# Two routed stages' last expert done tile by tile, their sums read back inside the stage, shared weights as a ninth expert, rows transposed inside the next stage, first modulations loaded early

## What is computed

```python
gates = softmax(x_flat @ router_w + router_b)
_, topk_idx = top_k(gates, 2)                       # 8 experts, capacity 320 tokens each
buf = ...                                           # the tokens of each expert
h = gelu(einsum('ecd,edh->ech', buf, w1) + b1)      # 256 -> 1024
out = einsum('ech,ehd->ecd', h, w2) + b2            # 1024 -> 256
y = einsum('ned,ne->nd', gathered, weights)         # back to the tokens, weighted and summed
```

```python
gate_in = concat([full_agg, hp_agg, wp_agg])        # three means over parts of the sequence
gate_scores = softmax((gate_in @ gate_w + gate_b) * (1 + scale) + shift)
topk_w, topk_i = top_k(gate_scores, 2)
out = sum over e of w_be[:, e] * mask[e] * (gelu(c @ ew1[e] + eb1[e]) @ ew2[e] + eb2[e])
out = out + gelu(c @ sw1 + sb1) @ sw2 + sb2         # the shared expert
```

## Time and profile before

| what | value |
|---|---|
| median of three runs | 2343.88 us (2343.78 to 2346.67) |
| span of the profiled execution | 2341.6 us (the profile gives no other time of it; the median is 2.3 us more) |
| TensorE busy | 2027.8 us, 87% of the span |
| DVE busy | 1336.4 us, 57% |
| ScalarE busy | 981.6 us, 42% |
| GpSimd busy | 370.6 us, 16% |
| instructions | 33811 |

### The profile page before, as it was taken

The page is one execution under the profiler, slowest core; times in us unless marked ns, Lnnn a source line. Parts: engine busy times, 40 slices in busy tenths (PEclk is TensorE's granted clock), DMA queues, the critical chain, the costliest instruction groups (busy, mean ns, idle before and its releaser), DMA issues. The chain is left out here.

```text
span 2341.6 us, 33811 instructions
## 1 busy us (share of the span) xinstructions
PE 2027.8 (87%) x13199; PEld 1631.2 (70%) x13199; DVE 1336.4 (57%) x2445; ACT 981.6 (42%) x1942; POOL 370.6 (16%) x308
## 2 busy tenths in 40 slices
PE   6699699999899999999999895499946767698698
PEld 3499578888687888888888784388933555366465
DVE  2766447777674465474463213666527457365796
ACT  2235445655453454454454322145323336455332
POOL 1368101323100000000000002257720000000000
PEclk7799799999999999999999997699977866899899
DMA  2654212233014112111200110544345002010000
GB/s 82 221 158 121 49 37 95 88 107 105 6 39 119 33 40 61 33 39 61 35 14 10 38 42 2 171 145 114 80 98 156 2 2 55 18 55 3 0 10 27
DMA packets 111160, 150.45 MB, mean 64 GB/s; under 512 B 6856, under 2 KB 93431, under 8 KB 110616
## 3 DMA queue, kind: packets, MB, share of 16 engines
q1 hardware_dynamic: 99836, 130.14, 18.6%
q0 software_dynamic: 11168, 18.18, 3.9%
HBM read 124.08 MB, written 24.22 MB: 63 GB/s over the span
## 5 line engine op out<-in xcount | busy, mean ns | idle before, releaser
L1750 DVE TENSOR_TENSOR m_h_lo<-m_hf,m_h_hi 128x512 fp32r<-128x512 f32 x256 | 173.8, 691 | 310.9 <-ACT m_hf L1725 307.1
L1722 ACT ACTIVATE m_h_hi<-m_h_ps,m_bT 128x512 fp32r<-128x512 f32 x256 | 177.0, 691 | 366.8 <-PE m_h_ps L396 347.0
L641 POOL DMA_INDIRECT token_sums<-e_y,slot_row x56 | 183.8, 3282 | 104.8 <-DVE e_y L749 84.4
L1725 ACT ACTIVATE m_hf<-m_h_ps,m_bT 128x512 f32<-128x512 f32 x256 | 175.0, 684 | 0.0
L711 ACT ACTIVATE e_h_hi<-e_h_ps,e_b1T 128x320 fp32r<-128x320 f32 (+1 forms) x128 | 77.9, 609 | 163.1 <-PE e_h_ps L396 158.0
L1435 DVE TENSOR_TENSOR c_h_lo<-c_hf,c_h_hi 128x512 fp32r<-128x512 f32 x120 | 91.9, 774 | 87.5 <-ACT c_hf L1391 86.8
L772 DVE TENSOR_TENSOR e_h_lo<-e_hf,e_h_hi 128x320 fp32r<-128x320 f32 (+1 forms) x128 | 72.3, 582 | 112.0 <-ACT e_hf L714 112.0
L1284 POOL TENSOR_TENSOR cT<-cT,c_yg 128x128 f32 x88 | 77.3, 879 | 265.1 <-DVE c_yg L1453 252.0
L1388 ACT ACTIVATE c_h_hi<-c_h_ps,c_b 128x512 fp32r<-128x512 f32 x88 | 62.2, 706 | 106.5 <-PE c_h_ps L396 105.9
L396 PE MATMUL m_y_ps<-m_h_hi,l_w_1hi 128*128 128x512 f32 x256 | 100.3, 392 | 3.4 <-issue 3.4
L396 PE MATMUL m_y_ps<-m_h_hi,l_w_0hi 128*128 128x512 f32 x256 | 99.8, 390 | 1.4 <-ACT m_gT L1736 1.4
(11 more groups left out here) (664 smaller groups left out, 5446.2 us busy)
## 6 DMA issues: line engine op xcount, KB each, us to landing
cT<-in_L_ffn_W_dram SPq DMA_DIRECT2D x30, 1024.0 KB, 5.2
res<-in_L_cond_ew_dram SPq DMA_DIRECT2D x22, 1024.0 KB, 5.0
cT<-in_L_ffn_w_dram SPq DMA_DIRECT2D x16, 1024.0 KB, 5.6
res<-gates_rows SPq DMA_DIRECT2D x8, 1024.0 KB, 15.5
l_mod<-modulation_rows SPq DMA_DIRECT2D x16, 512.0 KB, 6.5
token_rows<-d_tok SPq DMA_DIRECT2D x2, 2112.0 KB, 10.2
token_sums<-res SPq DMA_DIRECT2D x2, 2048.0 KB, 7.5
res<-token_sums SPq DMA_DIRECT2D x8, 512.0 KB, 7.2
```

What stands on the lines that cost most here:

```text
L641: pool.indirect_dma_start(out=sums, out_offset=bass.IndirectOffsetOnAxis(ap=st.slot_row[0:r, e, j:j + 1], axis=0), in_=y[0:r, e % 2, j, :] ...
L1722: act.activation(hs[0][:, f, :], h_ps[:, f % HB, :], ACT.Relu, bias=bT[:, at:at + 1])
L1725: act.activation(hf[:, f % HB, :], h_ps[:, f % HB, :], ACT.Relu, bias=bT[:, at:at + 1]).then_inc(act_done, 1)
L1750: dve.tensor_tensor(hs[1][:, f, :], hf[:, f % HB, :], hs[0][:, f, :].bitcast(F32), ALU.subtract).then_inc(h_ready, 1)
```

## The change

The last expert (e = 7) of both routed stages is multiplied down tile by tile, in the order 0, 2, 1, 3; each tile is scaled and scattered as it is finished. SyncE issues the loads of the sums inside the routed stage's block, behind its wait for the last scatter. In `e0` the shared expert's weights become a ninth expert's: they are loaded into the raw buffers and split by DVE during the last expert, like any next expert's. The small loads of layer 1, and ScalarE's Silu and the load of its Gelu table, move to that block too. `l1_turn_phase` is gone: TensorE transposes the first block of rows ahead of the first unit, and the other three inside its `up`, behind groups 1, 3 and 5, into PSUM banks from which ScalarE and DVE copy them. Means and choice, the count, the lists and their spreading come later, in the order that the diff shows. In `e3` the raw buffers take the first four chunks of modulations (`FirstModulations`), as they come free during the last two experts; `l3_phase` then starts with the weights.

```diff
     def load_w1(self, sp, e):
-        sp.dma_start(self.w1[e % 2], self.W1[e].rearrange("(c p) f -> p c f", p=P)).then_inc(self.w1_in[e % 2], 16)
+        W1 = self.W1[e] if e < E8 else self.shared[0]
+        sp.dma_start(self.w1[e % 2], W1.rearrange("(c p) f -> p c f", p=P)).then_inc(self.w1_in[e % 2], 16)
...
     def load_w2(self, sp, e):
-        sp.dma_start(self.w2[e % 2], self.W2[e].rearrange("(c p) d -> p c d", p=P)).then_inc(self.w2_in[e % 2], 16)
+        W2 = self.W2[e] if e < E8 else self.shared[1]
+        sp.dma_start(self.w2[e % 2], W2.rearrange("(c p) d -> p c d", p=P)).then_inc(self.w2_in[e % 2], 16)
...
+    E_ALL = E8 + following.experts
+    tile_order = [j for j in range(0, J, 2)] + [j for j in range(1, J, 2)]
...
+    order_of = lambda e: range(J) if e + 1 < E8 else tile_order
...
-            for e in range(2, E8):
+            for e in range(2, E_ALL):
                 sp.wait_ge(w1_split, 2 * (e - 1))
                 raw.load_w1(sp, e)
                 sp.wait_ge(w2_split, 2 * (e - 1))
                 raw.load_w2(sp, e)
-            if shared:
-                shared.load(sp, w1_split, w2_split)
+            sp.wait_ge(b_turned, 1)
+            following.load(sp, st, w1_split, w2_split)
+            back.load(sp, st)
...
-                for j, (_, r) in enumerate(tiles):
-                    pool.wait_ge(scaled, e * J + j + 1)
+                for i, j in enumerate(order_of(e)):
+                    r = tiles[j][1]
+                    pool.wait_ge(scaled, e * J + i + 1)
                     pool.indirect_dma_start(out=sums, out_offset=bass.IndirectOffsetOnAxis(ap=st.slot_row[0:r, e, j:j + 1], axis=0),
                                             in_=y[0:r, e % 2, j, :], in_offset=None, compute_op=ALU.add).then_inc(y_out, 16)
...
+
+                def products(f, j):
+                    a, r = tiles[j]
+                    for i, (h, w) in enumerate(((0, 0), (0, 1), (1, 0))):
+                        last = pe.matmul(y_ps[0:r, j // 2, j % 2, :], hs[h][:, f, a:a + r], w2s[e % 2][w][:, f, :],
+                                         start=False, stop=(f == FC - 1 and i == 2), skip_group_check=True)
+                    return last
+
+                if e + 1 < E8:
+                    for f in range(FC):
+                        pe.wait_ge(h_ready, e * FC + f + 1)
+                        for j in range(J):
+                            last = products(f, j)
+                    last.then_inc(y_done, 1)
+                else:
+                    for i, j in enumerate(tile_order):
+                        if i >= 2:
+                            pe.wait_ge(scaled, e * J + i - 1)
+                        for f in range(FC):
+                            if i == 0:
+                                pe.wait_ge(h_ready, e * FC + f + 1)
+                            last = products(f, j)
+                        last.then_inc(y_done, 1)
...
+            following.prepare(act, st)
...
-                dve.wait_ge(y_done, e + 1)
-                for j, (_, r) in enumerate(tiles):
+                for i, j in enumerate(order_of(e)):
+                    r = tiles[j][1]
+                    if i == 0 or e + 1 == E8:
+                        dve.wait_ge(y_done, e + i + 1)
                     if e >= 2:
                         dve.wait_ge(y_out, 16 * (e - 1) * J)
                     dve.tensor_scalar(y[0:r, e % 2, j, :], y_ps[0:r, j // 2, j % 2, :], taken[0:r, e % 3, j, D + e:D + e + 1],
...
             for e in range(E8):
-                more = e + 1 < E8
+                more = e + 1 < E_ALL
...
+                if e + 1 < E8:
+                    rows_lo(e + 1)
                 if more:
-                    rows_lo(e + 1)
                     w2_low(e + 1, 0)
                     w2_low(e + 1, 1)
             scale(E8 - 1)
...
+    def prepare(self, act, st):
+        act.activation(self.act_cond[:, :, :], st.condT[:, :, :], ACT.Silu)
+        act.activation(self.warm[:, :], st.ones[:, 0:1], ACT.Gelu_apprx_tanh)
...
-def l1_turn_phase(nc, sem, st, src, dst, back, shared, small, w1, w2):
...
-            def up(u):
+            def turn(b):
+                pe.wait_ge(back.res_in[b], 16)
+                if b >= 2:
+                    pe.wait_ge(rows_kept, b - 1)
+                for c in range(KC):
+                    for j in range(TPB):
+                        last = pe.transpose(y_ps[:, b % 2, c, j * P:(j + 1) * P], st.res[:, b * TPB + j, c * P:(c + 1) * P],
+                                            st.ident[:, :])
+                last.then_inc(rows_turned, 1)
...
+                    if f in between:
+                        between[f]()
...
+                if u == 0:
+                    pe.wait_ge(late_kept, 1)
...
+            turn_biases()
+            turn(0)
+            up(0, {1: lambda: turn(1), 3: lambda: turn(2), 5: lambda: turn(3)})
             down(0)
-            pe.wait_ge(selected, 1)
-            pe.matmul(ps[:, 0, 0:E4], st.ones[0:B, :], chosen[:, :], start=True, stop=True, skip_group_check=True)
-            pe.matmul(ps[0:B, 0, E4:2 * E4], st.tri[0:B, 0:B], chosen[:, :], start=False, stop=True,
-                      skip_group_check=True).then_inc(counted, 1)
-            up(1)
-            pe.wait_ge(listed, 1)
-            for e in range(E4):
-                last = pe.matmul(ps[:, 1, 0:2 * ROUTED * SLOTS], st.ones[0:B, :], hot[:, e, :, :].rearrange("b w s -> b (w s)"),
-                                 start=(e == 0), stop=(e == E4 - 1))
-            last.then_inc(spread, 1)
+            gate_logits()
+            up(1, {4: count_chosen})
+            pe.wait_ge(counts_kept, 1)
+            down(1)
+            up(2, {2: spread_list})
             pe.wait_ge(columns_set, 1)
-            down(1)
-            for u in range(2, UNITS):
+            down(2)
+            for u in range(3, UNITS):
                 up(u)
...
+            act.wait_ge(rows_turned, 1)
+            act.activation(xs[0][0][:, :, :], y_ps[:, 0, :, :], ACT.Copy).then_inc(x_hi, 1)
             act.wait_ge(b_kept, 1)
+
+            def keep_rows(b):
+                act.wait_ge(rows_turned, b + 1)
+                act.activation(srcT[:, :, blk(b)], y_ps[:, b % 2, :, :], ACT.Copy).then_inc(late_kept, 1)
...
+                    if u == 0 and f == 4:
+                        keep_rows(2)
+                    if u == 0 and f == 6:
+                        keep_rows(3)
...
-            dve.tensor_scalar(agg[:, 1:3, :, :], agg[:, 1:3, :, :], with_proprio, None, ALU.mult).then_inc(agg_done, 1)
+            keep_rows(0)
...
+                if f == 1:
+                    keep_rows(1)
             x_low(1)
...
+            means()
+            choose()
...
+                if f == 3:
+                    keep_counts()
+            list_slots()
             x_low(2)
...
-            for u in range(2, UNITS):
+            for f in range(FC):
+                h_low(2, f)
+                if f == 0:
+                    out_shared(1)
+                if f == 4:
+                    set_columns()
+            x_low(3)
...
+    experts = 0
...
+    def load(self, sp, st, w1_split, w2_split):
+        for c in range(4):
+            sp.wait_ge((w1_split, w2_split)[c % 2], 2 * (E8 - 1 + c // 2))
+            for a in range(2):
+                src = self.ada_rows.rearrange("(t a) n -> a t n", a=2)[a, c * CHUNK:(c + 1) * CHUNK, SH_MSA:SH_MSA + 2 * D]
+                sp.dma_start(self.rows[c][a * S:(a + 1) * S, :, :], src.partition_broadcast(S)).then_inc(self.mod_in[c], 16)
...
             def modulation(c):
-                if c >= 2:
+                if c >= 6:
                     sp.wait_ge(v_done, CHUNK * (c - 1))
-                rows(mod[:, c % 2, :, :], c, SH_MSA if c < 4 else SH_MLP, mod_in[c % 2])
+                rows(mod[:, c % 2, :, :], c, SH_MLP, mod_in[c % 2])
...
-            modulation(0)
-            back.load(sp, st)
-            modulation(1)
             for i, name in enumerate("qkv"):
                 weight(w_qkv[:, :, i * D:(i + 1) * D], w["w_" + name], qkv_in)
                 bias(b_qkv[:, i * D:(i + 1) * D], w["b_" + name], qkv_in)
-            modulation(2)
-            modulation(3)
             weight(w_o[:, :, :], w["w_o"], wo_in)
             bias(b_o[:, :], w["b_o"], wo_in)
             gate(0)
...
             def stretch(m):
                 t, k = m % NT, m // CHUNK
-                dve.wait_ge(mod_in[k % 2], 32 * (k // 2 + 1))
+                if k < 4:
+                    dve.wait_ge(first_mods.mod_in[k], 32)
+                else:
+                    dve.wait_ge(mod_in[k % 2], 32 * ((k - 4) // 2 + 1))
```

More of the change, by code:

```diff
@@ L787, in _ @@
             scale(E8 - 1)
-    return y_out, 16 * E8 * J
+    return back
 class State:
@@ L1194, with l1_cond_phase @@
 ROUTED = (PICKED * B + E4 * (SLOTS - 1)) // SLOTS
[L1197 removed]
+def l1_cond_phase(nc, sem, st, srcT, accT, w1s, w2s, small, back, ew1, ew2, next_w1, next_w2, next_small):
     HB = 4
@@ new lines, in count_chosen, with spread_list @@
```

(28 more changed lines are left out.)

284 lines of the change are left out of this document (139 added, 145 removed).

## The result

| kernel | median | range | ratio to the kernel before |
|---|---|---|---|
| before | 2344.21 us | 2339.32 to 2346.67, 8 runs | |
| changed | 2351.12 us | 2349.3 to 2359.07, 8 runs | 1.0034 (95%: 1.0021 to 1.0047) |

The account below looks back on a forecast made before the run. It took the chain from the routed stages' last scale through scatters, landing, block change and loads to first use as the bound. -14.0 (layer 3) and -7.2 (layer 1) gave -21.2, from 2343.88 to 2322.7 us; range 2314 to 2332.

Parts of the forecast that it names:

- chain of waits: At both routed stages' ends: scale, scatters, landing, block change, loads, first use; each microsecond removed saves one of the kernel.
- left out the dense stages, which the change doesn't touch: Scope of the reading of waits: dense stages were excluded as untouched, with no term in the sum.
- The rival on the slower side: Layer 1's first units: TensorE's clock stays low longer, losing 19 us a unit; two units give 2361 us; chance 0.04.
- Layer 2 to layer 3, -14.0: Layer 3's start: statistics begin at about 1732.4 instead of 1746.43 through earlier scatters and loads, -14.0 us.
- The weights come in time: Layer 3's first big product: rival had query, key and value weights landing late, gain there only 11, 2325.7 us; chance 0.14.
- Layer 0 to layer 1, first product -8.9: Layer 1's start: first product at 262.4 instead of 271.33, -8.9 us; with later terms this half sums to -7.2.
- the forecast's 4.0 us: Loads of the sums: time the first quarter needs to arrive when nothing runs beside it, 4.0 us.
- Transposes +3.5: Layer 1's first unit: 24 transposes moved inside it, where TensorE is the bound, cost +3.5 us.
- wait -1.8: Before layer 1's second unit's down products: the 1.80 us wait goes, as lists are spread in the third, -1.8 us.
- the 0 to +2 us kept for them: Layer 1's second unit: allowance in the range for means, gate and choice coming later, 0 to +2 us.
- Scatters held by casts alone: Layer 0's end: rival where subtractions don't hold scatters; some 2 us more gain, 2320.7 us; chance 0.14 for scatters held less.
- The new block did open without waiting for the loads: Both block changes: rival had opening wait for SyncE's loads, first use some 5 us later each, 2333 us; chance 0.07.

Follow-up runs that it names:

- e2: Kernel before, with an unused 4-byte tile ahead of layer 1's x and h tiles, moving them 32 bytes: 2376.47 us, ratio 1.0125.
- e5: Changed kernel, with scratch tile `warm` laid into an unused part of the gate weights' tile, so x and h start as before: 2322.12 us, ratio 0.989.
- e12: e5 without the early modulations: layer 3 loads its first four chunks itself, as before: 2326.06 us, ratio 0.9918.
- e6: e5 with the ninth set's splits moved behind the last expert's low halves, ScalarE making the high halves: 2314.93 us, ratio 0.9862.
- e8: Kernel before, with an unused 256-byte tile ahead of layer 1's x and h tiles: 2347.5 us, ratio 1.0001.
- e1: Changed kernel, with scratch tile `warm` widened from 4 to 64 bytes per partition: 2348.17 us, ratio 1.0016.
- e4: e1 with 4-byte tiles between the x and h tiles of both layer 1 stages, h 32 bytes off: 2356.17 us, ratio 1.0041.
- e9: Kernel before, with an unused 128-byte tile ahead of layer 1's x and h tiles: 2369.65 us, ratio 1.0112.
- e3: Kernel before, with 4-byte tiles ahead of and behind layer 1's split weights (weights 32, x and h 64 bytes on): 2372.54 us, ratio 1.0119.
- e10: Kernel before, with only layer 1's split weights moved 32 bytes, x and h on multiples of 256: 2374.04 us, ratio 1.0131.
- e11: Kernel before, with 64 unused bytes between the x and h tiles of layer 0's routed stage: 2360.23 us, ratio 1.0073.

## Why the prediction was wrong

Its chain of waits was right at nearly every link; what failed is something that it took for granted.

- *Failed: it "left out the dense stages, which the change doesn't touch".* That put layer 1's 4512 big products at before's speed, a term of nothing in the sum. They took 6.6 ns more each, some 30 us, because their operands start elsewhere. e2 shows the loss without the change, e5 the change without the loss. The allocation was neither a term nor a bound nor a rival. The rival on the slower side had TensorE slow down, but by its clock; the granted clock was 1.00 in both windows. Why the start has a price stays open.
- *Layer 2 to layer 3, -14.0: measured -14.7.* The loads go out 3.9 us behind the last scatter's start (1746.81 to 1750.66, forecast 3.8). The statistics start when the new block opens; the profile names TensorE's sequencer as what released them, and not the rows. GpSimd's last scatter ended at 1748.35, and the block opened 6.4 us behind it, where 6.3 were forecast. The weights come in time: the product of 1767.75 waits for ScalarE alone. e12 shows how thin that is.
- *Layer 0 to layer 1, first product -8.9.* Measured -7.1, with the last expert 1.6 us later at that: -8.7. The first scatter was put at 11.2 us and took 11.09; the last was put at 250.5 and started at 252.09, 1.6 us later like all else. The block opened 5.6 us behind the last scatter's end (253.65 to 259.25), where 5.2 were forecast; by the forecast's 4.0 us the rows landed at 259.8, so the two lay 0.5 us apart instead of 1.
- *Transposes +3.5, wait -1.8.* The 24 took 3.1 us of busy time; the wait for the column list is gone, and no other stands in its place in the first three units. The gate's products stand at 291.7 and the count at 299.88 without a wait of TensorE, so the 0 to +2 us kept for them were 0. From layer 1's first product to layer 2's last scale e5 takes 1452.0 us and before 1451.7 (1723.05 - 271.33), so all this gave back 0.3 us where the sum had +1.7; what brought the rest wasn't followed up.
- *The rivals.* Scatters held by casts alone: the first scatter ended 1.4 us behind the last subtraction and 4.1 behind the last cast (237.62 + 1.21 = 238.83), where this rival wanted 1.5 behind the cast. That speaks for the forecast, and e6 shows the price of where the splits stood, 7 us, for casts and subtractions together. The Trainium skill (page "SBUF — State Buffer", section "Who interferes with whom") infers that `tensor_tensor` leaves the making of descriptors alone. The traces disagree: beside subtractions alone a scatter took 2.65 us instead of 1.43, and 3.30 instead of 1.55 in e6. The new block did open without waiting for the loads. The clock was no worse: the first 4 us behind layer 1's first product were granted 0.50 before and after the change, and from 6 us behind it both had 1.00.
- With the loss taken out (e5) the forecast's number came, 2322.1 for 2322.7. That it fits within 1 us is in part luck: on that chip the gain is 25.7 us by the medians and 19.6 by the traces, with 21.2 forecast. The places agree better: layer 3's first big product came 20.5 us earlier.

## What to carry to other kernels

A new tile, of 4 bytes even, moves every tile allocated behind it; before a change is forecast, list the starts of the operands in the dense stages, before and after, and where one differs, time the old kernel with an unused tile that moves it by as much (e2). When a stage slows in which nothing was changed, count its instructions in a window: at the same granted clock, fewer in the same busy time means that each is slower. And work on DVE that is "free" because DVE idles is not free for GpSimd's scatters and gathers beside it (11.09 us against 2.27 in e6): put it where as few as possible are under way.

## What the hardware showed that was not expected

Products of 512 columns at full clock, by the starts of weights, x and h modulo 256 bytes, from the windows of 900 to 1100 us (200 us over the count; busy throughout; the mean distance of starts within a group is some half a ns more in each kernel, since the count takes in the products at both edges):

| kernel | weights | x | h | products | ns each |
|---|---|---|---|---|---|
| before, e5, e8 | 0 | 0 | 0 | 884 | 226.2 |
| e1 | 0 | 64 | 64 | 876 | 228.3 |
| e4 | 0 | 64 | 96 | 867 | 230.7 |
| e9 | 0 | 128 | 128 | 863 | 231.7 |
| changed, e2 | 0 | 32 | 32 | 859, 858 | 233 |
| e3 | 32 | 64 | 64 | 859 | 232.8 |
| e10 | 32 | 0 | 0 | 858 | 233.1 |

Moving either operand costs time, and the order isn't that of a power of two. For products of 256 columns with h as the stationary operand 64 beyond was the quicker place (115.5 against 119.3 ns, e11). In layer 0's routed stage of the changed kernel x and h start 32 beyond as well, and there that costs next to nothing: its 320-column products stand 147 ns apart in both kernels, its 256-column ones 119.4 to 119.6 against 119.3. What decides it, the starts themselves or their distance, and why, stays open; the table holds for these tiles and shapes, and e9's row for the feed-forward part alone.
